# A post-norm layer with recurrent time mixing and a routed expert network, on one core: layer norms applied by ScalarE with a ready-made shift in place of VectorE

## The reference

```python
def time_mix(x, ln_w, ln_b, Wk, Wv, Wr, Wo):              # two such layers, one behind the other
    n = layer_norm(x) * ln_w + ln_b
    k, v, r = n @ Wk.T, n @ Wv.T, sigmoid(n @ Wr.T)
    state[t] = 0.95 * state[t-1] + 0.05 * (k * v)[t]
    return x + (r * state) @ Wo.T

x = layernorm(x + time_mix(time_mix(x)))                  # norm 2 below: its result is x_ln
logits = x @ router_w + router_b                          # 8 experts, top 2, softmax of the two
einp = scatter x into its two experts' slots, 307 slots an expert and sequence
h, g = einp @ w_c_fc + b_c_fc, einp @ w_gate + b_gate     # 128 -> 512
o = silu(h * g) @ w_c_proj + b_c_proj                     # 512 -> 128
x = layernorm(x + p0 * o[e0, slot0] + p1 * o[e1, slot1])  # the final norm
```

## Time and profile before

| | |
|---|---|
| median of 3 runs | 401.93 us (401.17 to 403.64) |
| the profiled execution | 401.28 us, of which 399.5 us span |
| busy: TensorE, VectorE, ScalarE, GpSimd | 323.6, 268.3, 159.7, 208.3 us |
| mean granted TensorE clock | 0.919 of full speed |

### The profile page before, as it was taken

The page is one execution under the profiler, slowest core; times in us unless marked ns, Lnnn a source line. Parts: engine busy times, 40 slices in busy tenths (PEclk is TensorE's granted clock), DMA queues, the critical chain, the costliest instruction groups (busy, mean ns, idle before and its releaser), DMA issues.

```text
span 399.5 us, 6793 instructions
## 1 busy us (share of the span) xinstructions
PE 323.6 (81%) x2171; PEld 273.0 (68%) x2171; DVE 268.3 (67%) x846; ACT 159.7 (40%) x292; POOL 208.3 (52%) x245
## 2 busy tenths in 40 slices
PE   6876866777999999999999999998899888895000
PEld 3433454245988979998897998897798887894000
DVE  6698967387866878968687787782456675752134
ACT  2525411112654453555544454342554544451000
POOL 4446844875035463334556648456466558300674
PEclk9998756888999999999999999899999999999555
DMA  7763184114013113311111432132163132121112
GB/s 225 222 58 105 53 256 128 39 42 136 2 37 88 36 52 103 85 38 38 47 49 46 121 88 73 29 92 79 46 173 82 40 99 71 51 58 32 39 53 66
DMA packets 53058, 31.73 MB, mean 79 GB/s; under 512 B 12704, under 2 KB 48807, under 8 KB 53024
## 3 DMA queue, kind: packets, MB, share of 16 engines
q1 hardware_dynamic: 47840, 22.99, 20.9%
q0 software_dynamic: 4096, 8.06, 7.2%
q10 hardware_dynamic: 1088, 0.26, 0.3%
HBM read 18.92 MB, written 12.71 MB: 79 GB/s over the span
## 4 chain that ended last, share of the span: by engine, by line
PE 54%; DVE 14%; issue 11%; POOL 10%; DMA 4%; ACT 3%; another core or an unknown queue 2%; POOLq 0%; SPq 0%; DVEq 0%; ACTq 0%
PE ps_o L622 16%; POOL picked L1114 4%; POOL slot_rows L1084 3%; PE pair0g L608 2%; PE bank L489 2%; PE pair0g L610 2%; PE pair1g L608 2%; DVE prod L998 2%; PE bank L499 2%; PE bank L497 2%; PE bank L469 2%; PE pair0g L609 2%; PE pair0h L610 2%; PE pair0h L608 2%
## 5 line engine op out<-in xcount | busy, mean ns | idle before, releaser
L622 PE MATMUL ps_o<-proj_sb,hidden 128*104 128x128 f32 x768 | 97.7, 275 | 4.1 <-DVE o_sb L1007 2.1
L1084 POOL DMA_INDIRECT slot_rows<-x_ln,row_to x64 | 71.2, 1112 | 48.1 <-DVE prod L998 27.0
L622 PEld LDWEIGHTS ps_o<-proj_sb,hidden 128*104 128x104 f32 x768 | 90.9, 171 | 6.2 <-issue 3.1
L1114 POOL DMA_INDIRECT picked<-expert_rows,row_from x64 | 66.4, 1037 | 54.0 <-issue 19.3
L735 ACT ACTIVATE gate_s<-pair0g,bgate_sb 128x308 f32<-128x308 f32 x64 | 33.0, 516 | 83.6 <-PE pair0g L610 71.8
L998 DVE SCALAR_TENSOR_TENSOR prod<-pair1h,bfc_sb,gate_s 128x308 f32<-128x308 f32 x64 | 33.9, 530 | 27.2 <-ACT gate_s L735 16.0
L998 DVE SCALAR_TENSOR_TENSOR prod<-pair0h,bfc_sb,gate_s 128x308 f32<-128x308 f32 x64 | 34.0, 531 | 24.7 <-ACT gate_s L735 18.5
L742 ACT ACTIVATE hidden<-prod 128x616 f32<-128x616 f32 x64 | 45.5, 711 | 9.5 <-DVE prod L998 7.7
L735 ACT ACTIVATE gate_s<-pair1g,bgate_sb 128x308 f32<-128x308 f32 x64 | 32.9, 515 | 26.4 <-PE pair1g L610 23.0
L608 PE MATMUL pair1g<-slotT_hi,gate_hi 128*128 128x308 f32 x64 | 26.5, 414 | 6.2 <-DVE prod L998 4.2
L608 PE MATMUL pair0g<-slotT_hi,gate_hi 128*128 128x308 f32 x64 | 25.9, 404 | 3.9 <-DVE prod L998 2.9
(11 more groups left out here) (148 smaller groups left out, 722.7 us busy)
## 6 DMA issues: line engine op xcount, KB each, us to landing
slot_x<-slot_rows SPq DMA_DIRECT2D x20, 256.0 KB, 3.4
expert_rows<-o_sb SPq DMA_DIRECT2D x32, 156.0 KB
x_in<-in_L_attn_h SPq DMA_DIRECT2D x4, 512.0 KB, 5.4
prod<-in_L_ffn_w_gate SPq DMA_DIRECT2D x8, 256.0 KB, 2.7
prod<-in_L_ffn_w_c_fc SPq DMA_DIRECT2D x8, 256.0 KB, 3.1
proj_sb<-in_L_ffn_w_c_proj SPq DMA_DIRECT2D x8, 256.0 KB, 5.9
out<-picked SPq DMA_DIRECT2D x16, 128.0 KB, 2.1
slot_rows<-slot_x SPq DMA_DIRECT2D x5, 256.0 KB, 4.5
```

The costliest lines, as they stand in the source:

```text
L622: mm = nc.tensor.matmul(ps_o[0:PART, P * part:P * part + P], hidden[:, e % 2, c, PART * part:PART * part + PART], proj_sb[:, e, c, :], sta ...
L1084: nc.gpsimd.indirect_dma_start(out=slot_rows, out_offset=bass.IndirectOffsetOnAxis(ap=row_to[:, c:c + 1], axis=0), in_=x_ln[:, b % RING, c ...
L1114: nc.gpsimd.indirect_dma_start(out=picked[:, j, k, :], out_offset=None, in_=expert_rows[b % 2], in_offset=bass.IndirectOffsetOnAxis(ap=row ...
```

## The change

The halves that are applied inside the periods (halves 4 and 5 of sequence 1 and all six of sequences 2 and 3, 14 halves of 4 tiles) and all 16 quarters of the final norm move from VectorE to ScalarE: 88 instructions in all. ScalarE computes `rstd * x + shift`. GpSimd makes `shift = -mean * rstd` by two more instructions for each half or quarter, one ahead of and one behind those it had. The halves applied in the head stay on VectorE. In the tables, half 1 goes from point 9 to point 8 and half 3 from point 19 to point 18; a quarter of the final norm keeps its point. Cut to its core:

```diff
-SCALAR_MIX = {9: [("turned", 0)], 10: [("kr", 0)], 12: [("turned", 1)], 13: [("kr", 1)], 19: [("turned", 2)],
-              20: [("kr", 2)], 21: [("turned", 3)], 23: [("kr", 3)]}
-SCALAR_ROUTE = {2: [("turned", 4)], 4: [("turned", 5)], 6: [("lead", 0)]}
-VECTOR_MIX = {6: [("norm", 0)], 9: [("norm", 1)], 11: [("mix", 0)], 14: [("mix", 1)], 15: [("add", 0), ("stats", 2)],
-              16: [("norm", 2)], 17: [("add", 1)], 18: [("stats", 3)], 19: [("norm", 3)], 20: [("skip_sum", 0)],
+SCALAR_MIX = {6: [("norm", 0)], 8: [("norm", 1)], 9: [("turned", 0)], 10: [("kr", 0)], 12: [("turned", 1)],
+              13: [("kr", 1)], 16: [("norm", 2)], 18: [("norm", 3)], 19: [("turned", 2)], 20: [("kr", 2)],
+              21: [("turned", 3)], 23: [("kr", 3)]}
+SCALAR_ROUTE = {0: [("norm", 4)], 1: [("norm", 5)], 2: [("turned", 4)], 4: [("turned", 5)], 6: [("lead", 0)]}
+SCALAR_COMBINE = {13: [(1, 0)], 31: [(1, 1)], 6: [(2, 2)], 9: [(2, 3)]}
+SCALAR_COMBINE_LAST = {6: [(2, 2)], 9: [(2, 3)], 13: [(1, 0)], 17: [(1, 1)], 21: [(1, 2)], 25: [(1, 3)]}
...
+def on_scalar(b, n):
+    return max(0, step(b, n) - (8 if n < 4 else 2))
...
+            def norm_of(b, n):
+                norm, half = divmod(n, 2)
+                r, last = b % 2, n // 4
+                act.wait_ge(shift_made[last], on_scalar(b, n))
+                if not last and step(b, n) > 2:
+                    act.wait_ge(turned_ps[0], step(b, n) - 2)
+                dst = x_ln[:, b % RING, :, :] if last else normed
+                for j in range(HT * half, HT * half + HT):
+                    i = nc.scalar.activation(dst[:, j, :], source_of(b, n)[:, j, :], ACT.Identity,
+                                             bias=shift[:, r, norm, j:j + 1], scale=rstd[:, r, norm, j:j + 1])
+                i.then_inc(normed_made[last], 1)
+
+            def final_norm(b, q):
+                act.wait_ge(y_shift_made, nth(b, QUARTERS, q + 1))
+                for j in range(QT * q, QT * q + QT):
+                    i = nc.scalar.activation(picked[:, j, 0, :], picked[:, j, 1, :], ACT.Identity,
+                                             bias=y_shift[:, j:j + 1], scale=y_rstd[:, j:j + 1])
+                i.then_inc(y_normed, 1)
...
                 pool.wait_ge(moments_made[last], step(b, n))
+                if on_scalar(b, n):
+                    nc.gpsimd.tensor_scalar(shift[:, r, norm, tiles],
+                                            moments[:, r, norm, tiles, 0:1].rearrange("p j o -> p (j o)"),
+                                            -1.0, None, ALU.mult)
...
                   .then_inc(rstd_made[last], 1)
+                if on_scalar(b, n):
+                    pool.wait_ge(rstd_made[last], step(b, n))
+                    nc.gpsimd.tensor_tensor(shift[:, r, norm, tiles], shift[:, r, norm, tiles],
+                                            rstd[:, r, norm, tiles], ALU.mult).then_inc(shift_made[last], 1)
```

More of the change, by code:

```diff
@@ L109 @@
 VECTOR_AHEAD = {27: [("stats", 0)], 31: [("stats", 1)]}
[L110 to L118 removed]
+VECTOR_ROUTE = {4: [("top", 0)], 5: [("top", 1), ("choice", 0)], 8: [("rows", 0)]}
+VECTOR_COMBINE = {10: [(1, 0)], 29: [(1, 1)], 3: [(2, 2)], 7: [(2, 3)]}
+VECTOR_COMBINE_LAST = {3: [(2, 2)], 7: [(2, 3)], 10: [(1, 0)], 14: [(1, 1)], 18: [(1, 2)], 22: [(1, 3)]}
 POOL_MIX = {15: [("rstd", 2)], 17: [("rstd", 3)], 26: [("rstd", 4)], 31: [("rstd", 5)]}
@@ L209, in time_mix_moe @@
         rstd = sb("rstd", [P, 2, 3, TILES])
+        shift = sb("shift", [P, 2, 3, TILES])
         normT = sb("normT", [P, T])
@@ L349, in time_mix_moe, with source_of @@
         expert_view = [rows.rearrange("(e i p) d -> e p i d", i=PARTS, p=PART) for rows in expert_rows]
+        def source_of(b, n):
+            return (x_in, x_mid, x_in)[n // 2][:, b % 2, :, :]
         block = ctx.enter_context(nc.Block())
@@ L711, in lead @@
                 nc.scalar.activation(gap_t[:, :], gap[:, :], ACT.Tanh, scale=0.5).then_inc(gap_turned, 1)
-            stages = {"turned": turned, "kr": kr, "lead": lead}
+            def norm_of(b, n):
[15 more added lines that the diff above has]
+                i.then_inc(y_normed, 1)
+            stages = {"turned": turned, "kr": kr, "lead": lead, "norm": norm_of}
             def copy_slots(b, g):
@@ L756, in period @@
                         silu(b, e, 0)
+                    for behind, q in (SCALAR_COMBINE if b + 1 < B else SCALAR_COMBINE_LAST).get(point, ()):
+                        if b >= behind:
+                            final_norm(b - behind, q)
                     if b + 1 < B:
@@ L787, in _ @@
             silu(B - 1, E - 1, 1)
+            for q in range(QUARTERS):
+                final_norm(B - 1, q)
         @block.vector
         def _(dve):
-            def source_of(b, n):
-                return (x_in, x_mid, x_in)[n // 2][:, b % 2, :, :]
             def stats_of(b, n):
@@ L978, in gather_sum @@
                 i.then_inc(y_moments_made, 1)
-            def final_norm(b, q):
-                dve.wait_ge(y_rstd_made, nth(b, QUARTERS, q + 1))
-                dve.wait_ge(y_moments_made, nth(b, QUARTERS, q + 1))
-                for j in range(QT * q, QT * q + QT):
-                    i = nc.vector.tensor_scalar(picked[:, j, 0, :], picked[:, j, 1, :], y_moments[:, j, 0:1],
-                                                y_rstd[:, j:j + 1], ALU.subtract, ALU.mult)
-                i.then_inc(y_normed, 1)
-            combine_stages = {"gather_sum": gather_sum, "final_norm": final_norm}
             def product(b, e, j):
@@ L1023, in period @@
                             slots_low(b + ahead, g)
-                    for name, behind, q in (VECTOR_COMBINE if b + 1 < B else VECTOR_COMBINE_LAST).get(point, ()):
+                    for behind, q in (VECTOR_COMBINE if b + 1 < B else VECTOR_COMBINE_LAST).get(point, ()):
                         if b >= behind:
-                            combine_stages[name](b - behind, q)
+                            gather_sum(b - behind, q)
                     if b + 1 < B:
@@ L1047, in _ @@
             copy_out(B - 1, E - 1)
-            for name, q in VECTOR_TAIL:
-                combine_stages[name](B - 1, q)
+            for q in range(QUARTERS):
+                gather_sum(B - 1, q)
         @block.gpsimd
@@ L1123, in final_rstd @@
                     pool.wait_ge(y_normed, nth(b, QUARTERS, 0))
+                nc.gpsimd.tensor_scalar(y_shift[:, tiles],
+                                        y_moments[:, tiles, 0:1].rearrange("p j o -> p (j o)"),
+                                        -1.0, None, ALU.mult)
                 nc.gpsimd.tensor_scalar(y_shifted[:, tiles],
@@ L1129, in final_rstd @@
                   .then_inc(y_rstd_made, 1)
+                pool.wait_ge(y_rstd_made, nth(b, QUARTERS, q + 1))
+                nc.gpsimd.tensor_tensor(y_shift[:, tiles], y_shift[:, tiles], y_rstd[:, tiles], ALU.mult)\
+                  .then_inc(y_shift_made, 1)
             def pace(b, point):
```

15 lines of the change are left out of this document (5 added, 10 removed).

## The result

The changed kernel takes 425.97 us (median of 4 runs, 423.85 to 427.74), the one before, timed beside it, 402.64. The ratio is 1.057, with a 95% interval of 1.053 to 1.062: slower by 23 us. The profiled execution took 427.72 us, with a span of 426.0 and a mean granted clock of 0.897. Timed a second time in the experiments, the ratio was 1.062 (1.055 to 1.069).

The account below looks back on a forecast made before the run. TensorE was taken to bound periods 0 and 1. Terms 11.2 + 2.0 + 1.5 + 1.9 + 1.0 - 1.0 + 1.9 = 18.5 us on the profiled 401.28 gave 419.8, 420.4 as median; range 411 to 429.

Parts of the forecast that it names:

- entry of period 0: Start of period 0: halves 4 and 5 in ScalarE's queue put `turned` of half 4 and TensorE 1.5 us later.
- points 16 to 20, the wait, two periods: Middle of periods 0 and 1: `turned` of half 2 queues behind half 3, delaying TensorE's `kvr` 5.6 us each, 11.2.
- the clock behind the gaps: After TensorE's two gaps in periods 0 and 1: matmuls at half clock for a while, 1 us each, 2.0 together.
- entry of period 1: Start of period 1: ScalarE has room because TensorE's projection of three parts lies there, so nothing is lost.
- entry of period 2: Start of period 2: GpSimd's late rstd and shift for half 5 make gate copy, silu and `turned` 1.9 us later.
- gain in period 2, entry of period 3: Period 2: two final-norm quarters leaving VectorE gain 1.0 us; period 3's start: a quarter ahead of silu costs 1.0.
- last combine: End of kernel: GpSimd's four quarters take 1.6 us each, and ScalarE's last instructions are longer; 1.9 us lost.
- (a): Rival: waits are short, the two-pointer instruction takes the lower price and the clock stays up; 412.7 us, chance 0.12.
- (b): Rival: GpSimd's added product costs as much as the power, 5.6 us more, 426; chance 0.12 shared with (c) upwards.
- (c): Rival: ScalarE's 5.2 us remote wait at 279.90 comes once more (426) or vanishes (416); upwards shares 0.12 with (b).
- (d): Rival: VectorE bounds the kernel where TensorE was seen to, so the change is faster, 398 us; chance 0.03.
- (e): Rival, no change: ScalarE's and GpSimd's additions hide except at the end, or another step was as late; 402 to 404, chance 0.03.

Follow-up runs that it names:

- shift_applied_by_vector: The kernel before with GpSimd making shift as in the changed kernel, but VectorE applying x * rstd + shift at its old points; 409.12 us, ratio 1.011.

## Why the prediction was right, and where its sum was not

The forecast was 420.4 us with a range of 411 to 429; it came out at 425.97. Term by term, against the profiled execution (26.4 us longer, 18.5 forecast):

| term | forecast | measured |
|---|---|---|
| ahead of the first gate copy | none | 0.3 |
| entry of period 0 | 1.5 | 1.5 |
| points 16 to 20, the wait, two periods | 11.2 | 5.7 + 5.7 = 11.4 |
| the clock behind the gaps | 2.0 | 3.0 + 2.5 = 5.5 |
| entry of period 1 | 0 | -0.2 |
| entry of period 2 | 1.9 | 2.4 |
| gain in period 2, entry of period 3 | -1.0 + 1.0 | 3.3 from there to the last copy |
| last combine | 1.9 | 2.2 |

**The wait was right, by its own steps.** Four two-pointer instructions hold the queue for 1.55 us (136.66 to 138.21; 1.5 forecast), and one of L731 takes 482 ns (480). Half 2 started at 136.66, 0.06 behind the forecast 134.8 with the lag of 1.8, so shift came 0.6 us after rstd, as reckoned. Half 3 started at 144.57, 1.87 behind the forecast 142.7 with a lag of 1.8 on entering; `kvr` came 5.7 later than it had, for 5.6. The swap of one entry and the return of the two halves show that the order in ScalarE's queue causes it, and `shift_applied_by_vector` that GpSimd's delay by itself doesn't (0.3 us a period). The estimate by the Trainium skill ("VectorE: DVE Perf Modes", the section on the TRN2 errata), 293 ns for 128 columns, is measured for the plain copy, 301; with two pointers it is 488, and the larger sum was the nearer.

**The clock was mis-sized.** The step that failed is "Between nothing and 2 us each; I take 1". The gap was 4.26 us as forecast (4.4) and the clock fell just ahead of the restart, as the profile's windows show; but it then stayed low for 6 us behind the restart in the profiled execution and for 4 in the second trace, which makes 3.0, 2.5, 1.8 and 1.8 in place of 1. The rows at hand, those behind the last matmul, showed how the clock falls, not how long it takes to come back. The rule of the Trainium skill ("TensorE: Matmul & The Clock Gate", Part 1), that an idle TensorE falls to half clock, is what the trace shows (0.50 in the windows behind the gap), and the filled gap, at 1.00, shows the converse.

**Periods 2 and 3 lacked terms.** The gain of 1.0 was right (1.0 and 0.9 measured alone). The entry of period 3 was forecast at 1.0 for a quarter of the final norm ahead of gate copy and silu; the lag does rise there by 1.2 (21.8 to 23.0), but falls back to 21.9. Two things are missing in the sum. The first is the third wait of TensorE, at the stall of period 2: the lag rises by 2.7 us from point 16 to 24 (2.4 in the second trace, 3.3 in `shift_applied_by_vector`), and the cause stays open. The second is GpSimd's queue. I priced its two added instructions where a norm waited for their result, at the last combine and the entries, and not for the transfers that stand behind them. At the one place that was followed through they put off a gather by 0.87 us and, by VectorE's gather sum and product, made TensorE's wait 1.25 us longer; on the faster chips they are part of the late load of slots.

By the profiled executions the sum is 7.9 us short. That the median lies only 5.6 from the forecast is partly luck of the execution: the profiled one is 1.75 us above its median, and the second trace of the changed kernel is only 22.4 us longer than the one before, not 26.4.

**The rivals.** (a), short waits, is out: 488 ns and the fallen clock. (b), a product as dear as the power: it is 0.20 us long. (c) is out as it was put: with the change, ScalarE waits 5.36 us for something remote at 301.81 (with 2.73 ahead of it, at 295.32) and 4.60 at 298.21 in the second trace, the kernel before 5.20 and 5.18; it neither came a second time at its full length nor went. But it cost TensorE more, as said. The stall goes with the chips on which the kernel before is the slower, and not with the kernel: none of the eight traces from the faster chips has such a wait of 1 us or more. (d) and (e) stood on TensorE being covered, which the two gaps refute. The forecast of what the profile would show was met for the two gaps, the wait for shift at half 3 (3.98), L731 and the combine, whose quarters stand 1.66 to 1.73 us apart (1.6). It was not met in that the longest wait of TensorE in the periods is a third one (4.37), and VectorE's idle time grew by 48 us, not 30.

## What to carry to other kernels

Ahead of giving a relieved engine's work to another, ask who stands behind it in the new queue and who waits for that one: an instruction that waits for its operand holds up everything behind it, and the same work one place further down cost less than half as much. Price the small helper instructions in each queue they enter, also for the transfers behind them, since a gather issued 0.9 us later reached the saturated engine here, through VectorE. And count a gap of the saturated engine with what comes behind it: here 4.3 us of standing still took a further 2 to 3 at half clock.
